# Moving two high parts and x-hat from VectorE to ScalarE, and the last z to TensorE, in a cross-attention block

## The reference

```python
tgt1 = layer_norm(x, g1, be1)
q, k, v = tgt1 @ Wq.T + bq, tgt1 @ Wk.T + bk, tgt1 @ Wv.T + bv      # 16 heads
p = softmax(q @ k.T / sqrt(HD) + (1 - mask) * -1e9)
tgt = x + (p @ v) @ Wo.T + bo + memory @ Wg.T + bg
tgt1 = layer_norm(tgt, g2, be2)
out = tgt + relu(tgt1 @ W1.T + b1) @ W2.T + b2
```

## Time and profile before

| | us |
|---|---|
| median of 3 runs | 1756.54 |
| lowest, highest run | 1755.94, 1760.69 |
| the profiled execution: its own time | 1759.22 |
| its span, from the first to the last instruction | 1757.3 |
| busy: TensorE, VectorE, ScalarE, GpSimd | 1684.2, 1509.3, 1393.1, 953.5 |
| granted TensorE clock, mean | 0.990 |

### The profile page before, as it was taken

How to read it: one execution, slowest core, us unless ns; L and a number is a source line. 1 busy time by engine, 2 the same in 40 slices (tenths; PEclk the granted TensorE clock), 3 DMA queues, 4 the chain that set the end, 5 groups by cost and what they waited for, 6 DMA issues and landing times. The chain is left out here.

```text
span 1757.3 us, 53486 instructions
## 1 busy us (share of the span) xinstructions
PE 1684.2 (96%) x17272; PEld 1643.0 (93%) x17272; DVE 1509.3 (86%) x7136; ACT 1393.1 (79%) x5506; POOL 953.5 (54%) x906
## 2 busy tenths in 40 slices
PE   6799999999999999999999999999999999999997
PEld 5699999999999999999999999999999999999997
DVE  7798898898888888888888888888888888888873
ACT  4788788788788788788788788788788787787782
POOL 5355545545545545555555555555555555555544
PEclk8899999999999999999999999999999999999999
DMA  5434444444444444444444444444444444444421
GB/s 187 130 124 138 140 131 138 131 139 132 134 142 130 137 140 130 136 141 131 136 145 128 136 142 131 135 142 132 134 139 136 133 141 135 128 146 135 128 91 37
DMA packets 258951, 233.77 MB, mean 133 GB/s; under 512 B 26992, under 2 KB 209136, under 8 KB 258672
## 3 DMA queue, kind: packets, MB, share of 16 engines
q1 hardware_dynamic: 258672, 230.35, 41.5%
HBM read 62.73 MB, written 16.78 MB: 45 GB/s over the span
## 5 line engine op out<-in xcount | busy, mean ns | idle before, releaser
L448 ACT ACTIVATE scores<-scores,row_min 128x128 f32<-128x128 f32 x2048 | 799.5, 406 | 37.1 <-DVE row_min L725 37.1
L874 POOL TENSOR_TENSOR hT_lo<-hid,hT_hi 128x512 fp32r<-128x512 f32 x256 | 339.6, 1327 | 687.7 <-DVE hT_hi L684 687.7
L725 DVE CUSTOM_DVE_ANT_0 scores<-score_ps,mask_bias 128x128 f32<-128x128 f32 x2048 | 467.8, 286 | 1.5 <-issue 1.1
L448 ACT ACTIVATION_READ_ACCUMULATOR scores<-scores,row_min 128x1 f32 x2048 | 420.5, 205 | 0.0
L460 ACT ACTIVATE probs<-turn_ps 128x512 f32<-128x512 f32 x512 | 306.3, 599 | 92.6 <-PE turn_ps L1022 92.6
L956 PE MATMUL ffn_ps<-w_hi,hT_lo 128*128 128x256 f32 x1024 | 301.2, 294 | 32.6 <-POOL hT_lo L874 32.2
L1022 PE MATMUL turn_ps<-ident,scores 128*128 128x128 f32 x2048 | 307.1, 273 | 5.3 <-ACT probs L460 5.3
L956 PE MATMUL ffn_ps<-zT_hi,w_lo 128*128 128x256 f32 x992 | 294.0, 296 | 1.4 <-ACT hid L501 1.2
L958 PE MATMUL ffn_ps<-w_hi,hT_hi 128*128 128x256 f32 x1024 | 284.2, 277 | 0.0
L957 PE MATMUL ffn_ps<-w_lo,hT_hi 128*128 128x256 f32 x1024 | 283.5, 277 | 0.0
L957 PE MATMUL ffn_ps<-zT_lo,w_hi 128*128 128x256 f32 x992 | 276.1, 278 | 0.0
(11 more groups left out here) (144 smaller groups left out, 4288.0 us busy)
## 6 DMA issues: line engine op xcount, KB each, us to landing
q_stack<-q_hi SPq DMA_DIRECT2D x128, 256.0 KB, 2.4
k_stack<-k_hi SPq DMA_DIRECT2D x256, 128.0 KB, 2.3
x_in<-x_dram SPq DMA_DIRECT2D x64, 256.0 KB, 2.7
mem_in<-memory_dram SPq DMA_DIRECT2D x64, 256.0 KB, 3.0
x_res<-x_dram SPq DMA_DIRECT2D x64, 256.0 KB, 3.0
q_stack<-q_lo SPq DMA_DIRECT2D x64, 256.0 KB, 2.3
k_stack<-k_lo SPq DMA_DIRECT2D x128, 128.0 KB, 2.3
inv<-inv_cols SPq DMA_DIRECT2D x256, 64.0 KB, 2.4
```

Source lines behind the costliest of these rows:

```text
L448: last = act.activation(exps, exps, ACT.Exp, bias=row_min[:, k, h:h + 1], scale=-1.0, accum_out=row_sum[:, k, h:h + 1])
L725: last = dve.tensor_tensor_reduce(out=scores[:, slot(i, t), h, :], in0=score_ps[t % 2][:, h * S:(h + 1) * S], in1=mask_bias[:, b, :], scal ...
L874: pool.tensor_tensor(halves[1], src, halves[0], ALU.subtract).then_inc(done, 1)
```

## The change

It makes four edits.

1. The high parts of the hidden quarters 2 and 3 (hT_hi) go from VectorE to ScalarE, where each stands directly behind its relu and waits for it. GpSimd's low parts of these quarters wait for the new semaphore.
2. x-hat, for the groups from iteration 0 on, is computed by ScalarE at tick 5, behind the high part of quarter 2, as Identity with scale = rstd and bias = -mean * rstd. GpSimd makes the bias with two more small instructions behind the inverse root. VectorE no longer computes x-hat; its 32x32 transposes of x move from tick 5 to tick 6 and wait for ScalarE.
3. The last z (group 63, iteration 64) is transposed by TensorE into PSUM between the third and the fourth down part, instead of by VectorE and four DMAs; ScalarE and VectorE split it from there.
4. The semaphores' counts follow, and GpSimd sets one more constant.

```diff
@@ act, iteration
                         last.then_inc(hid_relu, 1)
+                        if n >= 2:
+                            act.wait_ge(hid_relu, HJ * g + n + 1)
+                            act.activation(hT[0][:, 2 * n:2 * n + 2, :], hid[:, n % 2], ACT.Copy
+                                           ).then_inc(hid_late_hi, 1)
...
+                    if norm and i >= 0 and t == 5:
+                        act.wait_ge(ln1_shift, i + 1)
+                        for b in range(GB):
+                            last = act.activation(x_in[:, b, :], x_in[:, b, :], ACT.Identity,
+                                                  bias=shift1[:, b:b + 1], scale=rstd1[:, b:b + 1])
+                        last.then_inc(x_scaled, 1)
...
-                    if out_ and t == 12:
+                    if is_at(i, GROUPS) and t == 12:
+                        split_high(by_tile[1], zT[0][:], z_turned, 1, hid_ready, HJ * (GROUPS - 1), z_hi)
+                    elif out_ and t == 12:
@@ dve, iteration
-                    if ffn and t == 0:
+                    if is_at(i, GROUPS + 1) and t == 0:
+                        split_low(by_tile[1], zT, z_hi, GROUPS, z_split)
+                    elif ffn and t == 0:
...
-                    if ffn and t in HIDDEN_TICKS and t < 8:
+                    if ffn and t in HIDDEN_TICKS[:2]:
                         hidden_high(i - 2, HIDDEN_TICKS.index(t))
...
-                    if norm and t == 5 and i >= 0:
-                        layer_norm_apply(i + 2, x_in, mv1, rstd1, ln1_rstd, x_in, ln1_ready)
+                    if norm and t == 6 and i >= 0:
                         dve.wait_ge(x_cols, 16 * QUADS * (i + 1))
-                        turn_quads(x_blocks, x_in, ln1_ready, i + 3, x_blocked)
+                        turn_quads(x_blocks, x_in, x_scaled, i + 1, x_blocked)
...
                         layer_norm_apply(g, resid, mv2, rstd2, ln2_rstd, xhat2, ln2_ready)
-                        dve.wait_ge(attnT_split, g + 1)
-                        turn_quads(attn_blocks, xhat2, ln2_ready, g + 1, z_blocked)
-                    if ffn and t == HIDDEN_TICKS[-1]:
-                        hidden_high(i - 2, HJ - 1)
+                        if i < GROUPS:
+                            dve.wait_ge(attnT_split, g + 1)
+                            turn_quads(attn_blocks, xhat2, ln2_ready, g + 1, z_blocked)
@@ pool, iteration
                     if norm and t == 5:
-                        inverse_root(i + 2, mv1, var1, rstd1, ln1_mean, ln1_var, ln1_ready, ln1_rstd)
+                        if i >= 1:
+                            pool.wait_ge(x_scaled, i)
+                        inverse_root(i + 2, mv1, var1, rstd1, ln1_mean, ln1_var, ln1_ready, min(i + 2, 2), ln1_rstd)
+                        if i >= 0:
+                            pool.tensor_tensor(minus_mean[:], mv1[:, :, 0], minus_one[:], ALU.mult
+                                               ).then_inc(ln1_opposite, 1)
+                            pool.wait_ge(ln1_opposite, i + 1)
+                            pool.wait_ge(ln1_rstd, i + 3)
+                            pool.tensor_tensor(shift1[:], minus_mean[:], rstd1[:], ALU.mult
+                                               ).then_inc(ln1_shift, 1)
...
-                        split_low(hid[:, n % 2], [h[:, 2 * n:2 * n + 2, :] for h in hT], hid_hi,
-                                  HJ * g + n + 1, hid_split)
+                        split_low(hid[:, n % 2], [h[:, 2 * n:2 * n + 2, :] for h in hT],
+                                  hid_hi if n < 2 else hid_late_hi, 2 * g + n % 2 + 1, hid_split)
@@ pe, iteration, between up and down
+                    if is_at(i, GROUPS) and t == 12:
+                        pe.wait_ge(ln2_ready, GROUPS)
+                        pe.wait_ge(resid_ready, GROUPS)
+                        turn(by_tile[1], xhat2).then_inc(z_turned, 1)
```

More of the change, by code:

```diff
@@ L177, in xattn_block @@
         eps, minus_half = sb("eps", [P, GB]), sb("minus_half", [P, GB])
+        minus_one, minus_mean, shift1 = (sb(n, [P, GB]) for n in ("minus_one", "minus_mean", "shift1"))
         score_ps = [bank("score_ps0"), bank("score_ps1")]
@@ L204, in xattn_block @@
         x_turned, x_hi, x_split = sem("x_turned"), sem("x_hi"), sem("x_split")
+        x_scaled = sem("x_scaled")
+        ln1_opposite, ln1_shift = sem("ln1_opposite"), sem("ln1_shift")
         ln1_centred, x_blocked, x_cols = sem("ln1_centred"), sem("x_blocked"), sem("x_cols")
@@ L226, in xattn_block @@
             sem(f"ln2_{n}") for n in ("stats", "mean", "var", "rstd", "ready"))
+        z_turned = sem("z_turned")
         z_blocked, z_cols, z_hi, z_split = (sem(f"z_{n}") for n in ("blocked", "cols", "hi", "split"))
         hid_ready, hid_relu, hid_hi, hid_split = (sem(f"s_hid_{n}") for n in ("ready", "relu", "hi", "split"))
+        hid_late_hi = sem("s_hid_late_hi")
         down_ready, resid_biased, y_summed = sem("down_ready"), sem("resid_biased"), sem("y_summed")
@@ L387, in iteration @@
                     sp.dma_start(x_res[:], x_rows[i]).then_inc(xres_loaded, 16)
-                if out_:
+                if out_ and i < GROUPS:
                     sp.wait_ge(z_blocked, i)
@@ L778, in iteration @@
                         dve.wait_ge(x_loaded, 16 * (i + 3))
+                        if i >= 1:
+                            dve.wait_ge(ln1_shift, i)
                         layer_norm_stats(i + 2, x_in, stats1, mv1, ln1_rstd, ln1_stats, ln1_mean)
@@ L839, in _ @@
             pool.memset(one[:], 1.0).then_inc(constants_set, 1)
-            pool.wait_ge(constants_set, 3)
+            pool.memset(minus_one[:], -1.0).then_inc(constants_set, 1)
+            pool.wait_ge(constants_set, 4)
             def set_zeros(n):
@@ L860, in low_parts_and_zeros, with inverse_root @@
                 set_zeros(1)
-            def inverse_root(g, mv, var, rstd, mean_done, var_done, ready, done):
+            def inverse_root(g, mv, var, rstd, mean_done, var_done, ready, before, done):
                 pool.wait_ge(mean_done, g + 1)
                 if later(g):
-                    pool.wait_ge(ready, g)
+                    pool.wait_ge(ready, before)
                 pool.tensor_tensor(var[:], mv[:, :, 1], eps[:], ALU.add).then_inc(var_done, 1)
@@ L895, in iteration @@
                     if out_ and t == 7:
-                        inverse_root(i - 1, mv2, var2, rstd2, ln2_mean, ln2_var, ln2_ready, ln2_rstd)
+                        inverse_root(i - 1, mv2, var2, rstd2, ln2_mean, ln2_var, ln2_ready, i - 1, ln2_rstd)
                     if out_ and t == 3:
```

## The result

| | before | after |
|---|---|---|
| median, us | 1757.43 (4 runs, 1755.94 to 1760.69) | **1819.42** (4 runs, 1817.59 to 1823.22) |
| span of the profiled execution, us | 1757.3 | 1817.8 |

The ratio is 1.0353, 95% interval 1.033 to 1.0375: **3.5% slower**, 62 us, where 17 were forecast and 1790 was the top of the range. The direction was right, the size was not.

A forecast was written before the change was run, and what follows sets the result against it. TensorE was taken as the bound, with a 0.74 us hole a round; closing it but adding a 25.71 ring plus 0.96 clash gives 26.67 a round: 18 + 1 - 2.2 = +16.8, 1773 us, range 1712 to 1790.

The forecast's parts named there:

- Hole: TensorE's 0.74 us wait each round for GpSimd's fourth hT_lo; the change removes it, up to -44 us over 60 rounds.
- The ring: Loop from zT_hi through ScalarE's x-hat, VectorE, GpSimd's inverse root, xhat and DMAs to the next zT_hi: 25.71 us a round.
- I take 0.84, the same width: Time of the two x-hat Identities on ScalarE, taken from the relu pair: 0.84 us, ends 0.70 and 0.95.
- The budget of the Trainium skill: ScalarE at 0.3 us per ACTIVATE plus 0.83 ns an element: a round 0.3 longer, 17 us in all; not adopted.
- The price on top: GpSimd's fourth hT_lo, now right behind rstd, delays VectorE's xhat pair: 1.84 for 0.88, +0.96 us a round, ends 0 and 1.15.
- The first clash: GpSimd's fourth hT_lo running into VectorE's xhat pair on the ring: +0.96 us a round.
- Late landings: Wait for z's DMAs, mean 2.28 us, up to 3.5; with the full block a round of 26.95, 1790 us.
- The new ring: Loop closed by x-hat's move to ScalarE, because VectorE's transposes of x must wait for it: 25.71 us against TensorE's 25.62.
- Last z: At the kernel's end, TensorE transposes the last z instead of the DMAs: -2.2 us.
- The sum: 18 + 1 - 2.2 = +16.8 us on the profiled execution, added to the median 1756.5: 1773 us.
- Nothing on the path is gained: VectorE's two x-hat instructions (1.91 us) and two casts go, but transposes of x wait for ScalarE: no gain on the path.
- no clash: Rival, chance 0.20: xhat stays at 0.88 us, the round is 25.7, -44 us, 1712 us.

The follow-up runs named there:

- 25.6 by experiment: The changed kernel with GpSimd's xT_hi alone made to wait until VectorE has written xhat: 1793.79 us, 25.6 less than the changed kernel.
- both steps held: The changed kernel with GpSimd waiting, ahead of the fourth hT_lo and so of xT_hi behind it, until VectorE has written xhat: 1733.48 us.
- one added wait: The kernel before with GpSimd starting the second hT_lo only when VectorE has written x-hat: 1711.62 us, ratio 0.9731.
- the best version: The kernel before with x-hat on ScalarE and the last z on TensorE, the high parts left on VectorE: 1705.06 us.
- the kernel with the memsets: The kernel before with three GpSimd memsets of a spare tile added behind the second inverse root: 1763.85 us, ratio 1.0022.

## Why the prediction was wrong

- **Hole: right.** It closes (954.63 - 954.27 = 0.36 in the changed kernel). What it is worth was right too: TensorE's own round was forecast at 25.62, and the kernels in which nothing else binds have rounds of 25.60.
- **The ring: right in its links but one**, 25.71 forecast, 26.02 by the links measured with an undisturbed xhat. Of the 0.31, x-hat is 0.24. The step that was mis-sized is **"I take 0.84, the same width"** for x-hat: it takes 1.08, above the 0.95 that I gave as an end. The error is 0.24 x 60 = 14 us. The 394 ns of the set-up row, which I read as "with scale and bias", could not have told: its scale is the constant 0.0 in the instruction (`scale=0.0`), and only its bias is read from SBUF. The scale from SBUF is the operand that took 0.09 us each time, and the set-up's scores<-scores,vec, which I did not read, showed it before. The other links, 0.07 a round, are 4 us.
- **The budget of the Trainium skill** ("ScalarE: Activation LUTs", section "Rules for kernel authors"), 0.51 us for an Identity, I set aside because the relu and cast rows were shorter; 0.588 was measured, above both. That budget is given for an ACTIVATE whose bias is a pointer operand. The copy has no such bias, and there my row was right (0.63 against 0.72).
- **"The price on top": right in kind, and short by one.** The first clash was forecast at 0.96 and measured at 0.94 in the ordinary rounds. But the step asked only what hT_lo's earlier start does to xhat, and not what starts earlier behind hT_lo. In the earlier trace rows hT_lo begins after xhat and so keeps xT_hi, next on GpSimd, from any clash. With hT_lo gone from there, xT_hi runs into the second xhat whenever x's DMAs land early enough: 0.84 to 0.87 in 32 rounds, 27 us by the model, 25.6 by experiment. This is the largest term that the forecast lacks: it had xT_hi at nothing, without a reason.
- **Late landings** were named as an end: rounds of 28.6 to 29.1 have 5.2 to 5.7 us from the end of the transposes to zT_hi instead of 4.06. There are only a few of them, some 5 us in all.
- **The new ring was not needed.** The forecast has x-hat's move to ScalarE close the ring on which the clash is paid. The high parts alone, without it, are as slow (1821.76 us): there the clashes are paid on the ring through the scores and VectorE.
- **Last z: -2.2 forecast, -4 measured.** The forecast had TensorE's idle time and not the clock that fell after it.
- The sum, corrected by the rows: 16.8 + 14 (x-hat) + 4 (the other links) - 1 (the first clash) + 27 (xT_hi) + 5 (landings) - 2 (last z) = 64. It is 4 less, 60, as the rounds before average 26.44 and not the 26.37 from which the forecast's +0.3 starts. Measured: 62.
- **"Nothing on the path is gained" by freeing VectorE of x-hat: right in the changed kernel, and hiding the point.** x-hat alone gains 50 us, the last z 4, the high parts lose 63. They don't add up, as two of them close the same hole; once it is closed by x-hat, moving the high parts can only bring hT_lo and xhat together.
- The rival *no clash* had 1712 us. With both steps held it is 1733: it too lacked the 0.24 of x-hat (14 us), the other links (4) and the landings on the ring (7).

## What to carry to other kernels

An engine that releases work earlier also releases what is queued behind that work: follow the freed engine's queue at least two instructions on, against every VectorE instruction on the path with two SBUF inputs. A wait that makes GpSimd idle can be worth 2.7% (one added wait took the kernel before from 1759 to 1712 us), so look for pairs whose mean in one place is twice that of the same pair in another before moving work between engines. And when several edits are bundled, run each alone: here the best version is two of the three.

## What the runs showed of the hardware that I had not expected

- Two VectorE instructions in a row can each lose to a GpSimd instruction of their own: the pair takes 0.88 us undisturbed, 1.82 with one such neighbour and 2.66 with two, ending 0.28 after the second. So GpSimd gets in between two VectorE instructions that are issued back to back; no run shows VectorE keeping its turn there. But a VectorE instruction that has already begun is not held up: at x-hat in the kernel before, the first of the pair begins 0.16 ahead of hT_lo and takes its 0.48 in every round, and hT_lo takes 1.46 for its 1.29. The clash costs GpSimd 0.17 there.
- The instruction that is held up ends 0.28 after GpSimd's recorded end, which is less than an undisturbed xhat takes (0.48). Either it gets going some 0.2 before that end or it has done a part of its work before; the trace does not tell. In the pair of 1.82 the second instruction then adds 0.40.
- An Identity with a scale and a bias from SBUF took 588 to 607 ns for 128x256, with the bias alone 495, the relu from PSUM with a bias 486.
- The low part of z on VectorE (zT_lo, two inputs in SBUF) is held up as well, in every kernel here: 0.69 us undisturbed, 1.19 on average before, where it starts under GpSimd's resid_b in 61 of 64 rounds, and 1.43 in the changed kernel. No run keeps these two apart, so what it costs is not known.
- After an idle 2.74 us TensorE's granted clock fell to 0.73 and 0.59 in the next two stretches of 2.5 us in the kernel before, and stayed at 1.00 after the same pause in the kernel with the memsets; after an idle 1.38 us at the same place it stayed at 1.00 in all seven traces that have it.
